# Attention and FFN block on one core: batch 0's split on VectorE, batch 1's projections ten slots later, V at slots 0 and 2, the product with V in two steps

## What is computed

```
xn  = layernorm(x)
Q, K, V = xn @ Wq.T, xn @ Wk.T, xn @ Wv.T          # rotary embedding on Q and K
P   = softmax(causal(Q K^T / 4));   attn = (P V) @ Wo.T
ffn = fp8_roundtrip(xn) @ fp8_roundtrip(Wf).T + bias   # one scale over the whole of xn
out = x + attn + ffn
```

## Time and profile before

| | us |
|---|---|
| median of 3 runs (465.06 to 466.79) | 465.14 |
| the profiled execution | 465.83 |
| its span, first to last instruction | 463.4 |
| PE busy in it | 408.1 |
| DVE busy | 356.8 |
| POOL busy | 282.0 |
| ACT busy | 278.6 |

### The profile page before, as it was taken

The page is one execution under the profiler, slowest core; times in us unless marked ns, Lnnn a source line. Parts: engine busy times, 40 slices in busy tenths (PEclk is TensorE's granted clock), DMA queues, the critical chain, the costliest instruction groups (busy, mean ns, idle before and its releaser), DMA issues.

```text
span 463.4 us, 9406 instructions
## 1 busy us (share of the span) xinstructions
PE 408.1 (88%) x2911; PEld 232.8 (50%) x2911; DVE 356.8 (77%) x1372; ACT 278.6 (60%) x505; POOL 282.0 (61%) x284
## 2 busy tenths in 40 slices
PE   7906769988979998999899989999899999999976
PEld 7505534443545555565456545655555454454434
DVE  2987677999698877887788868887888778778313
ACT  2655755565764675577656665575656746656741
POOL 2675763457677678467856765778657755234750
PEclk9956897997999999999999999999999999999999
DMA  8759117533367149604853375525662387020111
GB/s 284 248 170 214 36 60 178 111 55 115 99 108 138 37 129 206 124 15 145 198 116 49 114 193 105 93 71 173 124 137 70 130 169 139 3 91 2 47 47 45
DMA packets 34049, 53.16 MB, mean 115 GB/s; under 512 B 4496, under 2 KB 30480, under 8 KB 31120
## 3 DMA queue, kind: packets, MB, share of 16 engines
q1 hardware_dynamic: 34000, 52.57, 46.1%
HBM read 35.52 MB, written 16.78 MB: 113 GB/s over the span
## 4 chain that ended last, share of the span: by engine, by line
PE 60%; DVE 16%; ACT 8%; issue 7%; DMA 4%; POOL 3%; SPq 1%; DVEq 0%; ACTq 0%; POOLq 0%
PE o_ps L931 14%; PE st_ps L844 12%; PE s_ps L864 9%; PE m_ps L829 7%; DVE scratch L600 7%; PE m_ps L873 6%; PE m_ps L896 6%; ACT prob L712 4%; PE m_ps L880 2%; DMA xnT<-x_dram 2%; PE m_ps L901 1%; DMA q_st<-shift 1%; DVE amax L538 1%; DVE rowmax L600 1%; PE m_ps L887 1%
## 5 line engine op out<-in xcount | busy, mean ns | idle before, releaser
L600 DVE CUSTOM_DVE_ANT_0 scratch<-s_ps,causal 128x512 bf16<-128x512 f32 (+3 forms) x512 | 220.4, 483 | 49.3 <-PE s_ps L864 49.0
L712 ACT ACTIVATE prob<-st_ps 128x512 f32<-128x512 f32 x320 | 175.0, 602 | 122.7 <-PE st_ps L844 122.0
L458 POOL TENSOR_SCALAR_AFFINE_SELECT prob<-prob 128x512 f32<-128x512 f32 (+1 forms) x160 | 90.2, 566 | 140.8 <-ACT prob L712 140.6
L864 PE MATMUL s_ps<-k_st,q_st 96*128 96x512 bf16 (+3 forms) x512 | 123.8, 304 | 23.8 <-DMA k_st<-qk_parts 14.3
L844 PE MATMUL st_ps<-q_st,k_st 98*128 98x128 bf16 (+3 forms) x512 | 123.8, 306 | 9.6 <-ACT prob L712 6.4
L931 PE MATMUL o_ps<-prob,v_sb 128*17 128x512 f32 (+3 forms) x1024 | 88.5, 440 | 1.2 <-POOL prob L458 0.7
L844 PEld LDWEIGHTS st_ps<-q_st,k_st 98*128 98x128 bf16 x512 | 40.4, 98 | 89.2 <-ACT prob L712 45.1
L864 PEld LDWEIGHTS s_ps<-k_st,q_st 96*128 96x128 bf16 x512 | 49.5, 99 | 51.4 <-DVE rowmax L600 16.7
L600 DVE DVE_READ_ACCUMULATOR2_ANT rowmax<- 128x1 f32 x512 | 40.8, 80 | 0.0
L931 PEld LDWEIGHTS o_ps<-prob,v_sb 128*17 128x17 f32 x1024 | 20.3, 96 | 39.4 <-issue 35.0
L313 POOL TENSOR_TENSOR parts<-rot,parts 128x1024 bf16<-128x1024 f32 (+1 forms) x16 | 32.6, 2041 | 2.4 <-ACT parts L698 2.4
(11 more groups left out here) (101 smaller groups left out, 514.1 us busy)
## 6 DMA issues: line engine op xcount, KB each, us to landing
qk_parts<-parts SPq DMA_DIRECT2D x16, 768.0 KB, 3.7
q_st<-qk_parts SPq DMA_DIRECT2D x15, 384.0 KB, 4.9
k_st<-qk_parts SPq DMA_DIRECT2D x15, 384.0 KB, 7.2
xnT<-x_dram SPq DMA_DIRECT2D x8, 512.0 KB, 8.7
q_st<-qk_parts SPq DMA_DIRECT2D x15, 256.0 KB, 3.8
k_st<-qk_parts SPq DMA_DIRECT2D x15, 256.0 KB, 8.3
x_res<-x_dram SPq DMA_DIRECT2D x7, 512.0 KB, 3.5
out_dram<-x_res SPq DMA_DIRECT2D x7, 512.0 KB, 3.0
```

What stands on the lines that cost most here:

```text
L458: eng.affine_select(out=ap, in_=ap, compare_op=ALU.is_ge, fill=0.0, base=0, pattern=pat, channel_multiplier=-1).then_inc(masked, 1)
L600: eng.tensor_tensor_reduce(scratch[:, at % 3, col:col + w], s_ps[at % 3][:, col:col + w], causal[:, T - w:T], 1.0, NEG, ALU.add, ALU.max, ...
L712: eng.activation(prob[u][:, half * T:(half + 1) * T], st_ps[ST_BANK[2 * s + half]][:, :], ACT.Exp, scale=SCALE).then_inc(exp_done, 1)
L864: mm = eng.matmul(bank[:, col:col + (qb + 1) * P], q_st[0:ROWS, n % 2, h, qb * P:(qb + 1) * P], k_st[0:ROWS, n % 2, h, 0:(qb + 1) * P], st ...
```

## The change

The change has six parts.

1. On SP, x of batch 1 is loaded ahead of cos and sin, which have a semaphore of their own (`cos_in`), so that PE's first projections wait for the weights alone.
2. On POOL and ACT, the split of the projection weights moves from behind batch 0's chain to the start. DVE takes over remainder and low of batch 0's Q; DVE takes three statistics ahead of batch 0's products instead of four, then three more, and the last two in slots -10 and -8.
3. Batch 0's parts are written one by one (`write_first`), high and middle as soon as they are there, each a third of the bytes.
4. Between the start and slot -10, PE issues 46 `keep_busy` matmuls in three pieces, the second and third after waits for `low_done` and `parts_out`.
5. Batch 1's projections move from slot -10 to slots -3, -2, 0 and 1, and its chain follows by a table of its own (`EARLY_CHAIN`).
6. In every batch the second half of V moves from slot 3 to slot 2, and `pv` has two steps, at offsets 3 and 6.

```diff
-OFFSETS = {("v", 0): 0, ("mt", 1): 1, ("v", 1): 3, ("o", 0): 23, ("o", 1): 24, ("o", 2): 25, ("o", 3): 26, ("mt", 2): 7,
+OFFSETS = {("v", 0): 0, ("mt", 1): 1, ("v", 1): 2, ("o", 0): 23, ("o", 1): 24, ("o", 2): 25, ("o", 3): 26, ("mt", 2): 7,
...
-TURN_SLOT = {3: -10, 4: -9, 5: -7, 6: -5, 7: -3}
+EARLY = {("qk", 0): -3, ("qk", 1): -2, ("qk", 2): 0, ("qk", 3): 1}
...
+EARLY_CHAIN = {("rotate", 0): -1, ("high", 0): -1, ("remainder", 0): 0, ("middle", 0): 0, ("low", 0): 1,
+               ("write", 0): 2, ("rotate", 1): 2, ("high", 1): 2, ("remainder", 1): 3, ("middle", 1): 3, ("low", 1): 4,
+               ("write", 1): 5, ("read", 0, 0): 3, ("read", 0, 1): 6, ("read", 1, 0): 8, ("read", 1, 1): 9}
+TURN_SLOT = {3: -LEAD, 4: -LEAD + 1, 5: -LEAD + 2, 6: -LEAD + 4, 7: -LEAD + 6}
...
+            def write_first(w):
+                for t, (done, out_) in enumerate(((hi_done, early_out), (mid_done, early_out), (low_done, parts_out))):
+                    eng.wait_ge(done[w], 2)
+                    eng.dma_start(qk_dram[0, w].rearrange("t r j h n -> (j h) t r n")[:, t],
+                                  parts[:, w, t]).then_inc(out_[w], 16)
...
+            load_x(1)
+            eng.dma_start(cos_sb[:, :], cos).then_inc(cos_in, 16)
+            eng.dma_start(sin_sb[:, :], sin).then_inc(cos_in, 16)
+            for n in range(2, NB):
...
-            for n in range(3):
-                invert(n)
+            invert(0)
+            split_weights(0)
+            invert(1)
+            split_weights(1)
+            invert(2)
             eng.wait_ge(ln_rstd, 6)
             fill_ones(0)
             eng.wait_ge(consts, 7)
-            remainder(eng, 0, 0)
-            low(eng, 0, 0)
-            split_weights(0)
-            split_weights(1)
             split_x(1)
...
-            for n in range(4):
+            for n in range(3):
                 statistics(n)
-            eng.wait_ge(w_qk_in, 16 * 4)
+            eng.wait_ge(cos_in, 16 * 2)
             rope(0, 0, first_ps[0])
             rope(0, 1, first_ps[1])
             rotate(eng, 0, 0)
             rope(0, 2, first_ps[2])
+            remainder(eng, 0, 0)
             rope(0, 3, first_ps[3])
             rotate(eng, 0, 1)
+            low(eng, 0, 0)
             remainder(eng, 0, 1)
             low(eng, 0, 1)
-            for n in range(4, NB):
+            for n in range(3, 6):
                 statistics(n)
...
-                for kb in ((0,), (1, 3), (2,))[step]:
+                for kb, us in (((0, (0, 1)),), ((1, (2, 3)), (3, (2, 3)), (2, (4,))))[step]:
...
-                    eng.wait_ge(masked, SLOTS * n + 5 * g + (2, 4, 5)[step])
+                    eng.wait_ge(masked, SLOTS * n + 5 * g + (2, 5)[step])
...
-            keep_busy(26)
+            keep_busy(22)
             turn_rows(0)
-            keep_busy(8)
+            keep_busy(6)
             for k in range(4):
                 project_whole(k)
             turn_rows(1)
             turn_rows(2)
+            keep_busy(20)
+            eng.wait_ge(low_done[1], 2)
+            keep_busy(16)
+            eng.wait_ge(parts_out[1], 16)
+            keep_busy(10)
...
-                    for off, step in ((3, 0), (5, 1), (6, 2)):
+                    for off, step in ((3, 0), (6, 1)):
```

81 lines of the change are left out of this document (47 added, 34 removed).

## The result

The changed kernel takes 462.17 us (median of 20 runs, 459.67 to 466.42), the kernel before 465.1 in 20 runs beside it: a ratio of 0.9944, with a 95% interval of 0.9917 to 0.9972. It is faster by 2.9 us; I had forecast 456.3, a gain of 8.8. The profiled execution took 460.0, with a span of 458.3 (before 465.83 and 463.4), so it is a good one among its runs. A ratio compares a kernel with runs of the kernel before made beside it, slow ones left out, and can differ by 0.3% from the ratio of the two medians.

A forecast was written before the change was run, and what follows sets the result against it. PE bounds steady batches, DVE slots 10 to 20, neither slots -10 to 10. Gains of 7.0 (batches 1 to 5), 1.0 (batch 6), 0.8 less 0.4 (batch 7, end) and 0.4 (start) make 8.8: 456.3 us, range 450.5 to 465.

The forecast's parts named there:

- A memset doesn't hold a rotate of two SBUF inputs: Start: DVE's rotate runs freely beside POOL's memset of k_st and ends at 18.4; blocked, all that follows is 2.5 late.
- Slot 0's scores at 51.9, products done at 53.4: Slots -10 to 0 take about 17.5 us; slot 0's scores stand at 51.9 against 63.3, DVE's second product at 53.4.
- Slots 0 to 5, where ACT and POOL alternate: Batch 1's chain between exponentials uses up the lead: slot 5 at 76.4 against 78.5, low of K at 79.9.
- Slot 20 starts 0.4 earlier, no more: Slots 10 to 20: k_st lands at 90.4, DVE's first maximum is at 90.8 against 91.18, and DVE is the bound.
- Batch 1: First of batches 1 to 5, each forecast to gain the steady 1.4 us.
- The steady gain of 1.4 a batch, 47.5: Steady batches: 48.9 less 0.95, 1.05 and 0.5, plus 1.1 of new waits, makes 47.5; bounds of the gain 0.5 to 2.5.
- the join: Product with V in two steps: one step fewer in a group saves 0.24 us, 0.95 a batch.
- new waits: Steady batches: PE waits 0.6 in slot 0 and about 0.5 at slot 6 for exponentials, 1.1 a batch.
- the surviving lead: Rival, chance 0.13: half of what slot 0 gained at the start, about 6 us, stays; time 450.
- the vanished steady gain: Rival, chance 0.14: ACT paces the slots with one step less, and waits of 2.5 a batch take all; time 465.
- the slower case: Rival, chance 0.08: the moved step's 1.1 turns idle in slots 0, 5, 10 and 15; batch 50.8, time some 478.
- the memset: Rival, chance 0.15: POOL's memset holds DVE's rotate at the start; slot -10 at 36.5, time 458.8.

The follow-up runs named there:

- e11: The changed kernel with K's rotate, remainder and low of batch 1's chain on DVE instead of POOL, K's steps and write a slot earlier: 458.31 us, ratio 0.9865 to before.
- e2: The changed kernel without part 6, so parts 1 to 5 alone: 470.63 us, ratio 1.0118 to the kernel before.
- e1: The kernel before with part 6 alone (V at slot 2, product with V in two steps): 455.67 us against 464.61, ratio 0.9801.
- e3: The changed kernel with part 5 undone, batch 1's projections back in slots -10, -10, -7 and -5: 451.22 us, ratio 0.9706 to before.
- e12: e8 with the second half of V back at slot 3, the product with V still in two steps: 459.54 us, ratio 0.991 to before.
- e8: e7 with the second step with V waiting for masks key block by key block: 449.01 us, ratio 0.9675 to before.
- e9: The changed kernel with batch 1's chain spaced to one step a slot, low of K in slot 8 instead of 4: 462.16 us, ratio 0.9965 to before.
- e10: e8 with SP's write of Q's parts behind slot 0's extra rows, K's middle and low behind the exponentials: 445.89 us, ratio 0.9592 to before.
- e7: e3 with POOL's second memset of k_st moved from slot -7 to the start: 451.39 us, ratio 0.9723 to before.
- e5: The changed kernel with 45 more matmuls whose result nobody reads, in slots 1, 3 and 4: 462.73 us, ratio 0.9962 to before.

## Why the prediction was wrong

- **Slot -10 at 34.1:** 34.38. Right.
- **A memset doesn't hold a rotate of two SBUF inputs:** right. DVE's rotate ran 17.50 to 18.19, in 0.69, inside POOL's memset (15.85, 3.51), as the lock in the Trainium skill's "SBUF: two separate sides" (page "SBUF — State Buffer") has it:

```profile
17.50 0.69 DVE L317 TENSOR_TENSOR rot<-prod 128x512 f32<-128x512 f32 x1
```

- **Slot 0's scores at 51.9, products done at 53.4:** 53.0 and about 54.6, so 1.1 to 1.2 late. (The terms of the forecast, 34.1 and 17.5, make 51.6 and not 51.9.)
- **Slots 0 to 5, where ACT and POOL alternate:** the order came as written, wait by wait, and the sizes were too small. Low of K ends at 82.98, not 79.9. Of the 3.1, 1.1 stood already at slot 0, 0.4 are semaphores up to the copy of V (64.87, not 63.4), 1.2 is the projection at 1.2 GHz (2.90), a term that the sum did not have; 0.4 is spread over the rest. Slot 5 starts at 79.7, not 76.4.
- **"Slot 20 starts 0.4 earlier, no more": this step failed.** Slot 20 starts 2.3 later. It rested on `k_st` at 90.4 and DVE's first maximum at 90.8; they are at 93.21 and 94.70. The mis-sized term is the end of the chain, 3.1 late as just told; its transfers took 0.3 less than forecast. On top came 0.6 for the extra rows that queue behind the reads of `k_st`, for which I counted nothing. And I had no margin: in e11, where low of K ends 5.4 earlier, slot 10 starts 5.0 earlier. The true size of the start term is that of e2: parts 1 to 5 alone cost 5.5 us by the ratio, and 4.4 at slot 20; within them parts 1 to 4 gain 4.4 (e1 to e3) and part 5 costs 11. In the changed kernel part 6 gives 2.1 of these back before slot 20, which the forecast didn't count either. The range of 450.5 to 465 names this case ("a start of batch 1's K that is some us late") and holds the result; the likeliest case left it out.
- **Batch 1** was to gain 1.4 and loses 0.7: 51.86 against 51.17. It is 49.87 in e1. But that is no second loss. Slots 10 to 20 take 23.7 in the changed kernel and 26.6 in e1, so from slot 10 to slot 40 it is 75.6 against 76.5 (before 77.8): the changed kernel is 5.2 behind the one before at slot 10 and 3.0 at slot 40. DVE enters batch 1 with work of slots 10 to 20 unfinished (busy for 23.23 of 23.70). The stretch at 1.2 GHz that lies in slots 10 to 20 before and in e1 (granted clock 0.91) falls into slot 20 here: PE waits 1.47 for a maximum at 119.81, and V behind it takes 3.44 instead of 1.89. What is lost is all lost before slot 10.
- **The steady gain of 1.4 a batch, 47.5:** 47.35 to 47.45. The total is right, and the two groups of terms that e12 can tell apart are near: the wait for the copy of V with the idle time that goes with it is 1.25 (e12; forecast 1.05), and the join, the other idle time and the new waits make 0.3 together, where 0.95 + 0.5 - 1.1 = 0.35 was forecast. Those three can't be told apart by these runs, so the 0.24 for one step fewer isn't confirmed by the sum's coming out. New waits stand where they were expected, 0.71 at slot 1 (0.6) and 0.25 at slot 6 (0.5), and the step of 24 records takes 1.42 (268.81 to 270.23), as forecast.

```profile
267.67 0.39 PE L878 MATMUL st_ps<-q_st,k_st 98*128 98x512 bf16 x1 [0.71 <-ACT prob L744]
```

- **Batch 6** gained 2.0 (forecast 1.0), **batch 7** 0.7 up to slot 159 (0.8), and the end lost 0.8 (0.4), the part that e8 gives back.
- **The sum.** The profiled executions differ by 5.8 (465.83 and 460.0), forecast 8.8: 2.7 less at slot 20, 2.1 less in batch 1, 0.6 less in batch 7 and the end, against 1.7 more from batches 2 to 6 and 0.7 around the span. The medians differ by 2.9 only, because the profiled execution of the changed kernel is 2.2 below its median and that of the kernel before 0.7 above. Why its runs differ by up to 6.7 us stays open; the run at 466.42 had a mean granted clock of 0.956, that at 459.67 0.977, and the last slot told of with e8 is one place where 1.3 to 1.5 us of clock come and go between executions.

The rivals: the surviving lead didn't come, nor the vanished steady gain, nor the slower case. The result lies between the prices of the memset (458.8) and of the vanished steady gain (465), nearer to the latter, and by neither mechanism.

## What to carry to other kernels

A lead that is won ahead of a chain is worth only what still stands at the chain's last consumer: follow the moved work to its last landing, and compare that with the time of its first reader before the change, with all queues that it passes. Here starting the chain eight slots later cost 11 us although slot 0 came 7.6 earlier. The waits in between could be removed and nothing was gained as long as the chain still took 28 us (e9); when it took 23, 3.7 us came back (e11). Small transfers that gate the next slot are worth putting ahead of large ones in the queue, also when the large one isn't yet ready to be sent (e10).

## What was unexpected in the hardware

- The granted clock fell in and behind short waits, and on the path it was paid at once. In the changed kernel it is 0.50 from 61.9 on, inside PE's wait of 4.65, and again from 75.6 on, when PE had waited 1.80 (up to 74.64) and went on to wait 3.91; six matmuls then took 2.90 instead of 1.7. In e7 it fell behind a wait of only 1.81, in e5 with one of 4.99, and in e9 with one of 11.04, when PE ran at half clock up to about 98 (0.63 in that window). Filling the waits in slots 1, 3 and 4 with 45 matmuls held it at 1.00 to slot 5.
- Transfers of 4 KB took 1.7 to 2.0 us at the median between issue and landing in e3, e8 and e9 (those issued from 60 to 100 us), 3.4 and 2.9 behind the write of 768 KB in e8, and 5.4 and 5.5 behind reads of `k_st` in e5.
- In e11 DVE's steps of 128x1024 took 1.23 (remainder, with POOL idle until its last 0.2 us) and 1.65 (low, beside a mask of 0.64 on POOL); POOL's own take 2.13.
